# A decoder layer's self-attention: each tile's values placed directly behind its exponential sums and ahead of the next tile's scores, and the row gathers released by the spread of the reciprocals

## The reference, cut to what matters

```python
qkv = (x @ Wqkv + bqkv).reshape(B, M, 3, H, D)           # H = 16 heads of D = 32
...
qm = q[:, :, mrm, :] * scale                              # rows gathered by a fixed permutation
scores = jnp.einsum('bhnmd,bhnsd->bhnms', qm, Ksel)       # blocks of 64 queries, 32 keys each
sexp = jnp.exp(scores - jnp.max(scores, axis=3, keepdims=True))
acc = jnp.einsum('bhnms,bhnsd->bhnmd', sexp, Vsel)
lsum = 1e-06 + jnp.sum(sexp, axis=-1)
out = acc / lsum[..., None]
return out @ Wproj + bproj
```

## Time and profile before

| what | us |
|---|---|
| median of three runs | 1316.72 |
| the three runs | 1316.72, 1315.18, 1317.61 |
| span of the profiled execution | 1317.2 |

### The profile page before, as it was taken

One profiled execution on the slowest core, in us unless ns is written; L12 is line 12 of the kernel. 1 busy time (PEld: TensorE's weight loads), 2 busy tenths in 40 slices (PEclk: granted clock), 3 DMA queues, 4 the chain that ended last, 5 costly groups with the idle time before them and its releaser, 6 DMA issues.

```text
span 1317.2 us, 31656 instructions
## 1 busy us (share of the span) xinstructions
PE 1286.3 (98%) x12357; PEld 1042.3 (79%) x12357; DVE 937.1 (71%) x1879; ACT 668.0 (51%) x1868; POOL 413.6 (31%) x477
## 2 busy tenths in 40 slices
PE   8999999999999999999999999999999999999998
PEld 7978667777777788888888888888888886888886
DVE  6539778888776676777767777777776786665563
ACT  4447434333333655655556555565555663654552
POOL 3213445454442012213131222312211223455453
PEclk9999999999999999999999999999999999999999
DMA  8962142232323201103021021120202103665530
GB/s 263 325 227 65 58 154 81 84 98 75 107 87 124 81 9 41 49 17 105 17 73 50 18 87 36 41 81 9 73 25 89 65 10 129 228 195 177 177 104 22
DMA packets 69233, 123.75 MB, mean 94 GB/s; under 512 B 12313, under 2 KB 20529, under 8 KB 69090
## 3 DMA queue, kind: packets, MB, share of 16 engines
q1 hardware_dynamic: 60770, 98.17, 22.4%
q0 software_dynamic: 8320, 23.62, 5.1%
HBM read 83.19 MB, written 42.07 MB: 95 GB/s over the span
## 4 chain that ended last, share of the span: by engine, by line
PE 80%; DVE 9%; ACT 4%; DMA 4%; issue 2%; SPq 1%; POOL 0%; DVEq 0%; POOLq 0%; ACTq 0%
PE bank L71 18%; PE bank L73 16%; PE bank L72 16%; PE bank L2335 6%; PE bank L2323 6%; PE bank L2356 4%; PE bank L2348 2%; PE bank L1269 2%; PE bank L1299 2%; DMA raw<-in_L_xattn_Wkv_dram 1%; ACT b_prob L1640 1%; PE bank L1243 1%; DMA raw<-in_L_attn_Wqkv_dram 1%; PE bank L2407 1%; PE bank L2888 1%
## 5 line engine op out<-in xcount | busy, mean ns | idle before, releaser
L1640 ACT ACTIVATE b_prob<-bank,b_neg_top 128x155 f32<-128x155 f32 x496 | 187.3, 407 | 115.6 <-DVE b_neg_top L1852 106.1
L71 PE MATMUL bank<-turned_h,big_h 128*128 128x512 f32 x320 | 130.8, 409 | 1.1 <-DVE turned_l L2106 0.8
L73 PE MATMUL bank<-turned_h,big_l 128*128 128x512 f32 x320 | 125.3, 392 | 0.0
L72 PE MATMUL bank<-turned_l,big_h 128*128 128x512 f32 x320 | 124.9, 390 | 0.0
L1852 DVE TENSOR_REDUCE b_neg_top<-bank 128x6 f32<-128x930 f32 (+1 forms) x93 | 94.4, 1015 | 31.4 <-PE bank L2335 30.3
L71 PE MATMUL bank<-b_wo_h,b_ot_h 128*128 128x512 f32 x256 | 113.1, 442 | 0.2 <-DVE b_ot_l L1881 0.2
L2323 PEld LDWEIGHTS bank<-ident,b_prob 128*128 128x128 f32 x640 | 93.5, 191 | 19.8 <-issue 5.7
L2323 PE MATMUL bank<-ident,b_prob 128*128 128x128 f32 x640 | 103.2, 284 | 1.8 <-DVE b_pt L1869 1.0
L1640 ACT ACTIVATION_READ_ACCUMULATOR b_prob<-bank,b_neg_top 128x1 f32 x496 | 102.7, 207 | 0.0
L73 PE MATMUL bank<-b_wo_h,b_ot_l 128*128 128x512 f32 x256 | 101.7, 397 | 0.0
L1863 DVE TENSOR_TENSOR b_prob<-b_prob,b_recip 128x930 f32<-128x930 f32 (+1 forms) x93 | 98.2, 1056 | 3.2
(11 more groups left out here) (358 smaller groups left out, 3347.9 us busy)
## 6 DMA issues: line engine op xcount, KB each, us to landing
wide<-in_L_ffn_W_dram SPq DMA_DIRECT2D x16, 1024.0 KB, 5.2
slot_rows<-empty_row SPq DMA_DIRECT2D x8, 1032.0 KB, 14.7
a_xr<-in_x_dram SPq DMA_DIRECT2D x32, 256.0 KB, 2.6
x_scratch<-a_xr SPq DMA_DIRECT2D x32, 256.0 KB, 2.1
tiles<-x_scratch SPq DMA_DIRECT2D x32, 256.0 KB, 3.7
rows<-x_scratch SPq DMA_DIRECT2D x32, 256.0 KB, 3.5
out_dram<-rows SPq DMA_DIRECT2D x32, 256.0 KB, 2.0
rows<-slot_rows SPq DMA_DIRECT2D x7, 1032.0 KB, 8.0
```

The costliest lines, as they stand in the source:

```text
L71: pe.matmul(out, lh, rh, start=first, stop=False)
L72: pe.matmul(out, lh, rl, start=False, stop=False)
L73: return pe.matmul(out, ll, rh, start=False, stop=last)
L1640: last = act.activation(prob[:, n % 2, j, h:h + 2 * L2 - 1:2], s_banks[:, h, o:o + L2], ACT.Exp, bias=neg_top[:, n % 2, h, j:j + 1], accum ...
```

## The change

In `first`, `middle` and `last`, values(n) now stand directly behind sums(n). In `first` and `middle`, scores(n + 1) follow them directly, so one stretch of 64 matmuls on 32x32 pieces takes the place of two of 32. The waits on `s_shifted` and `a_norm` that this order makes needless go. POOL's gathers wait for the spread of tile n in place of its values.

```diff
-                hold(pool, s["a_done"], n + 1)
+                hold(pool, s["recip_spread"], n + 1)
                 for k in (2 * t, 2 * t + 1):
                     gather(G * (i + 2) + k)
...
-        def scores(n, mixed_before):
+        def scores(n, mixed_before=None):
             i, t = n // G, n % G
             pe.wait_ge(s["q_evac"], KD * (i + 1))
             hold(pe, s["k_ready"], n + 1)
-            hold(pe, s["s_shifted"], n)
-            hold(pe, s["a_norm"], mixed_before)
+            if mixed_before is not None:
+                hold(pe, s["s_shifted"], n)
+                hold(pe, s["a_norm"], mixed_before)
...
-        def values(n, shifted_before):
+        def values(n, shifted_before=None):
...
-            hold(pe, s["s_shifted"], shifted_before)
+            if shifted_before is not None:
+                hold(pe, s["s_shifted"], shifted_before)
...
             if tiled(n):
                 sums(n)
-                scores(n + 1, n)
+                values(n)
+                scores(n + 1)
             turn_x(i + 1, 3)
             if tiled(n - 1):
                 project(n - 1, 2, KD)
-            if tiled(n):
-                values(n, n + 2)
             queries(i + 1, 0, 0, 1)
...
         def middle(i, t, n):
             if tiled(n):
                 sums(n)
-                scores(n + 1, n)
+                values(n)
+                scores(n + 1)
                 project(n - 1)
                 spread_recip(n)
-                values(n, n + 2)
...
         def last(i, n):
             if tiled(n):
                 sums(n)
+                values(n)
             queries(i + 1, 5 if i + 1 == NG else 3)
             if tiled(n):
                 spread_recip(n)
-                values(n, n + 1)
                 project(n - 1)
```

## The result

The changed kernel takes 1326.84 us (median of four runs, 1326.23 to 1328.71); the kernel before, measured beside it, 1316.53 us. The ratio is 1.0077, with a 95% interval of 1.0064 to 1.0090: some 10 us slower, outside the range that was forecast. The profiled execution took 1326.23 us and its span is 1324.5 us.

The account below looks back on a forecast made before the run. PE was taken to bound the kernel (busy 98% of the span), with DVE the near second; terms -2.3 - 1.2 + 2.6 + 1.8 - 0.1 = +0.8 us gave 1317.5 us from a median of 1316.7, range 1311.5 to 1322.5.

Parts of the forecast that it names:

- The middle tiles' switches: Tiles t = 1, 2: one entry and exit of 32x32 pieces saved, 0.08 us lost behind the spread; -2.3 us in 16.
- The spread's wait: Tiles 9, 13, 17 and partly four others: the spread no longer waits for DVE's pieces; -1.2 us in all.
- Tiles t = 3: Seven tiles that a group follows: later spread and mix make the third transpose 0.37 us late; +2.6 us in all.
- Tiles t = 0: Seven tiles: later scores delay DVE's last split and the first query product; +0.25 us each, +1.8 us in all.
- Gathers: In t = 0 they wait for the spread, about 1.4 us later; claimed no direct cost on the path.
- In the sum these breaks stay as they are: PE's unexplained stops in the scores of tiles 2, 5, 6, 10, 14, 18, 22, about 7 us, were taken as unchanged.
- rival 2: Later t = 0 gathers bring 1.0 us breaks to six tiles t = 1: +6, 1323.5 us; 0.24, shared with later edges.

Follow-up runs that it names:

- e5: Changed kernel with 128 no-ops on PE ahead of the stage, which were dropped, making it a second sample of that kernel: 1328.75 us.
- e6: Kernel before with values directly behind sums in tiles t = 1 and 2 alone, gathers as before: 1320.45 us.
- e11: Changed kernel with 128 satisfied waits (64 instructions) at the start of PE's program: 1332.46 us.
- e4: Changed kernel without the gathers of groups 2 to 7: 1314.66 us.
- e3: Kernel before without the gathers of groups 2 to 7: 1314.42 us.
- e7: Kernel before with the gathers of t = 0 and t = 1 issued early, behind the scores of the next tile: 1317.96 us.
- e9: Kernel before with only the gathers of t = 1 issued early, those of t = 0 left behind the values: 1315.30 us.
- e12: e10 with the projection of the tile before placed between values and the next scores in the middle tiles: 1357.59 us.
- e10: Kernel before with values directly behind sums in tiles t = 1 and 2 alone and only the t = 1 gathers issued early: 1312.64 us.

## Why the prediction was wrong, point by point

**The middle tiles' switches (-0.14 each) were right in kind, too small.** Without a stop a middle tile takes 7.87 us for 8.14 at its best before, -0.27. The product behind the spread is late as predicted (228.46 to 228.68 to 228.99 in tile 9). Missed was that 64 values take 0.78 us to a 128x512 product but 0.65 us to the scores (252.49 to 253.14), so that leaving the 32x32 pieces costs 0.13 us more than the 0.11 read behind it. The rule of the Trainium skill that a change of mode drains the engine, "TensorEngine Tiling (Array Packing)", Tiling Modes, would by itself give 0.22 us and is nearer in size, but the 0.08 us behind the spread, which a step without a change of mode should not cost by that rule, are there.

**The spread's wait (-1.2) went as predicted**: the spread of tile 9 starts 0.24 us behind the last projection pass, and no window of t = 1 without a stop is above 7.87.

**Tiles t = 3 (+0.37 each) were mis-sized: +0.22.** Spread and mix did come 0.77 and 0.40 us later against the sums. DVE's timeline in tile 7, first before, then after:

```profile
207.05 0.68 DVE L1068 TENSOR_TENSOR a_mixed<-bank,a_recip_t 128x512 f32<-128x512 f32 x1
208.43 0.92 DVE L1073 TENSOR_TENSOR a_at_l<-a_mixed,a_at_h 128x512 fp32r<-128x512 f32 x1 [0.70 <-ACT a_at_h L927]
```

```profile
208.75 0.69 DVE L1068 TENSOR_TENSOR a_mixed<-bank,a_recip_t 128x512 f32<-128x512 f32 x1 [0.32 <-ACT a_recip_t L923]
210.15 0.73 DVE L1073 TENSOR_TENSOR a_at_l<-a_mixed,a_at_h 128x512 fp32r<-128x512 f32 x1 [0.70 <-ACT a_at_h L927]
```

The split of the projected rows took 0.92 us before and 0.73 after, and that gives back 0.2 of the 0.4 us. A duration read in one place was taken as fixed; it isn't. Before, POOL's bias addition (L867) still ran when the split began, until 208.80 us; after, it ended at 210.10, just ahead of the split at 210.15. Whether that is the cause was not tested.

**Tiles t = 0 (+0.25 each) were right**: 7.85 to 7.86 us for 7.57, with 0.72 us of idle time in front of the first query product in tile 8, for 0.26.

**Gathers ("cost on the path: none directly") and "In the sum these breaks stay as they are" are the steps that failed.** The sum of all other terms, forecast at +0.8, came out at about -0.3; the stops grew by 9.4. They did in two ways. The first is rival 2, at 0.24: the second gather of t = 0 moved over the stretch of t = 1, and short stops of 0.8 to 1.3 us came in six tiles that had no short ones, 5.4 us; in tiles 2, 6, to 22 the short stops went from 5.6 to 7.4 us, another 1.9. The prediction itself noted that a gather 1.7 us ahead of its scores does no harm and one at the scores does, and then left both in place, although the change moves the one by 1.5 us towards the stretch and makes the stretch beside the other twice as long. The second is the long stop: 0.42, 2.65 and 1.37 us in tiles 9, 12 and 24, where the kernel before has 1.37 in tile 5 and two small ones in the values of tiles 12 (0.62) and 20 (0.29), 2.2 us more in all. That makes the +9.4. In tile 12 the clock fell behind the stop (0.85 in the window), which goes with the 0.6 us by which its window exceeds an ordinary one and the stop; in e5 the same stop of 2.65 us left the clock at 1.00, and the window was 10.56 us for 11.15. The forecast of rival 2, 1323.5, is nearest, but it has only the first of the two ways and none of the long stops, on which the prediction says that no row shows them.

**What the long stop is.** Count PE's records in a trace (weight loads, matmuls and waits, in order of time). In all fourteen traces the long stops stand at record 193 or 194 of a block of 256, whatever the tile, and the short ones at any number. One packet of 0.02 MB on queue q8, "instruction", is fetched for each block, and lands 1.1 to 1.6 us before PE goes on, whether the stop is 0.2 or 2.8 us long. The DMA view of the changed kernel from 253.6 to 256.3 us:

```profile
GB/s 122 121 61 61 30 243 0 0 0 0 0 0 0 0 0 0 0 0 0 0 0 0 0 0 0 0 0 0 0 0 0 0 0 0 0 0 0 0 0 0
...
q8 instruction: 1, 0.02, 2.2%
```

Each column is 0.07 us, and a packet stands in the column of its start. The last thing that starts is the block itself, in the sixth column, at 254.0 us; it takes 0.93 us, nothing starts behind it, and PE goes on at 256.29, that is 2.29 us from the start of the fetch. This is the same everywhere. Over the 574 crossings that tiles 0 to 30 of the fourteen traces hold, PE never passed one sooner than 2.21 us after that block's fetch began. At 63 crossings it stopped for 0.16 us or more, and 62 of them lie 2.2 to 2.9 us behind the start of the fetch (one 3.3); where the fetch began over 3.4 us ahead, three stops are left, one with a gather beside it and two of 0.19 us. So the length of a long stop is what is missing of these 2.2 to 2.9 us.

A stretch of sums, values and scores has 272 to 283 instructions in some 1.8 us, so a block is used up in less time than the next takes to come, if its fetch begins only at the crossing before or later; in tile 12 that crossing was at 251.54 us, and the fetch began 2.5 us behind it. The Trainium skill, "Runtime: NRT & Kernel Launch", Instruction fetch mechanics, says that what crossing a 16 KiB boundary (256 instructions) costs is mostly hidden. In the 128x512 products the traces agree: in none does PE wait there without a cause; in a stretch of small ones it isn't, 2.77 us at worst (e6). The time from the fetch also tells why in e11 tile 26 stops and tile 29 does not: the fetch began 2.42 us before the crossing in the one and 3.53 us in the other. What sets the start of a fetch, which lies between 2.1 us ahead of the crossing before and 7.5 us behind it, is open, and with it why tile 24 stops in the changed kernel and not in e4.

**What the short stop is** stays in part open. e3, e4, e7 and e9 show that it needs a gather issued beside 32x32 products, that it goes with the gather, and that 128x512 products don't show it. Whether POOL's work for the descriptors, their transfers or something else holds PE was not separated: gathers of a smaller size were not tried.

## What to carry to other kernels

Joining stretches of small matmuls saves the switches between shapes (0.27 us a tile here), but PE can then use up its program faster than it is delivered, and a gather finds twice as long a stretch of small matmuls to fall on: count the instructions of a stretch, and look at what is issued beside it. A stop without a cause in the trace is a term of the sum like any other: before it is left "as it is", ask which of its conditions the change moves. Gathers from GpSimd belong beside large products; moving two of four there and leaving the edges of a group alone gave 1312.64 us, the best kernel of this study.

## What the hardware showed that was not expected

- PE passed from one block of 256 instructions to the next no sooner than 2.21 us after the fetch of the next began, in 574 crossings. Inside a 32x32 stretch, which uses up a block in some 1.7 us, that stopped PE for up to 2.77 us; a move of the whole program by 64 instructions moved the stops to other tiles.
- A gather issued by POOL beside 32x32 matmuls stopped PE for about 0.64 us from start to start, often with a second stop ahead of it, in values as well as scores; no gather of these traces stopped 128x512 products.
- 64 values take 0.65 us when scores of the same piece size follow, and 0.78 us when a full-array product does.
- After some stops the granted clock fell to the lower of its two levels, for 3.4 us in tile 12 (0.85 over its window) and in tile 13 of e12 (0.86); after the same stop of 2.65 us in e5 it did not.
- Executions of one kernel differ by several microseconds: e10's lay between 1311.18 and 1315.10 us. Why is open.
